# Adaptive-norm transformer pair on one core: TensorE's side stage ahead of the value products in each half step

## The reference

```python
# layer 0
score = (h @ Wq) @ (h @ Wk).T / sqrt(32);  causal, zero and masked -> float32 min
x = x + ga * softmax(score) @ (h @ Wvdown @ Wvup)
h = layernorm(x) * (1 + cb) + sb
x = x + gb * relu(h @ We[argmax expert] + be) * p       # one expert of 8 per token
# layer 1
q, k, v = h @ Wq.T, h @ Wk.T, h @ Wv.T                   # 16 heads of 8
x = x + ga * (softmax(q @ k.T * 8**-0.5) @ v @ Wout.T + bout)
x = x + gb * ((h @ W1.T + b1) @ W2.T + b2)
```

## Time and profile before

| | us |
|---|---|
| median of 3 runs | 1754.97 (1753.21 to 1757.65) |
| profiled execution, its own time | 1750.79 |
| span of its trace | 1749.5 |
| TensorE busy | 1605.5 |
| VectorE busy | 1491.2 |
| ScalarE busy | 1367.7 |
| GpSimd busy | 670.5 |

### The profile page before, as it was taken

How to read it: one execution, slowest core, us unless ns; L and a number is a source line. 1 busy time by engine, 2 the same in 40 slices (tenths; PEclk the granted TensorE clock), 3 DMA queues, 4 the chain that set the end, 5 groups by cost and what they waited for, 6 DMA issues and landing times.

```text
span 1749.5 us, 55041 instructions
## 1 busy us (share of the span) xinstructions
PE 1605.5 (92%) x23302; PEld 664.7 (38%) x23313; DVE 1491.2 (85%) x2256; ACT 1367.7 (78%) x1934; POOL 670.5 (38%) x1085
## 2 busy tenths in 40 slices
PE   5768999999999999999999999999999998998998
PEld 2543343334334343334334343334433343222224
DVE  4649988899889988899889988899888988998963
ACT  4443688887899778887898878897788878887884
POOL 2321345435534455335554264434554263002010
PEclk9899999999999999999999999999999999999999
DMA  2120211112210321112210321112111222101111
GB/s 72 51 65 25 63 39 41 35 54 61 67 50 17 96 65 42 30 44 75 66 48 19 82 65 52 34 40 83 45 40 35 60 59 66 35 25 50 36 29 32
DMA packets 83281, 87.10 MB, mean 50 GB/s; under 512 B 9452, under 2 KB 67484, under 8 KB 83036
## 3 DMA queue, kind: packets, MB, share of 16 engines
q1 hardware_dynamic: 82492, 83.07, 16.2%
q10 hardware_dynamic: 544, 0.52, 0.1%
HBM read 61.02 MB, written 21.99 MB: 47 GB/s over the span
## 4 chain that ended last, share of the span: by engine, by line
PE 59%; ACT 19%; DVE 13%; issue 5%; SPq 2%; DMA 1%; POOL 1%; ACTq 0%; POOLq 0%
PE pv_psum L836 20%; PE side_psum L564 14%; ACT p L1049 11%; PE buffer L821 11%; DVE row_max L1373 7%; PE buffer L811 7%; PE buffer L564 2%; PE side_psum L654 2%; PE side_psum L621 2%; SPq L539 2%; ACT s L965 1%; ACT o_sb L1058 1%; DVE st_f L1112 1%; DMA q_ops<-nm_rows 1%; ACT hT_b L1038 1%
## 5 line engine op out<-in xcount | busy, mean ns | idle before, releaser
L1373 DVE TENSOR_REDUCE row_max<-buffer 128x2 f32<-128x1024 f32 x1024 | 1234.0, 1219 | 142.8 <-PE buffer L811 132.0
L1049 ACT ACTIVATE p<-buffer 128x1024 f32<-128x1024 f32 x1024 | 1044.7, 1024 | 202.0 <-PE buffer L821 187.6
L836 PE MATMUL pv_psum<-p,v 128*9 128x256 f32 x8192 | 588.5, 384 | 10.6 <-ACT o_sb L1058 9.4
L811 PE MATMUL buffer<-k_ops,q_ops 24*128 24x512 f16 x2048 | 400.3, 388 | 34.0 <-ACT p L1049 25.0
L821 PE MATMUL buffer<-q_ops,k_ops 26*128 26x512 f16 x2048 | 400.7, 388 | 14.3 <-DVE row_max L1373 8.5
L836 PEld LDWEIGHTS pv_psum<-p,v 128*9 128x9 f32 x8192 | 150.4, 89 | 244.4 <-issue 161.4
L821 PEld LDWEIGHTS buffer<-q_ops,k_ops 26*128 26x128 f16 x2048 | 96.8, 91 | 382.2 <-issue 219.4
L1504 POOL TENSOR_TENSOR hm<-masks,hT_f 128x1024 f32<-128x1024 bf16 x56 | 120.3, 2148 | 102.3 <-PE side_psum L564 99.0
L811 PEld LDWEIGHTS buffer<-k_ops,q_ops 24*128 24x128 f16 x2048 | 96.8, 91 | 162.7 <-ACT p L1049 130.7
L1519 POOL TENSOR_SCALAR nm_parts<-nm 128x16 f16<-128x16 f32 x64 | 13.1, 205 | 293.9 <-DVE nm L1296 293.6
L564 PE MATMUL side_psum<-we,hm 128*32 128x128 f32 x3648 | 121.7, 275 | 2.7 <-issue 2.7
(11 more groups left out here) (309 smaller groups left out, 1621.1 us busy)
## 6 DMA issues: line engine op xcount, KB each, us to landing
masks<-masks_rows SPq DMA_DIRECT2D x16, 1024.0 KB, 6.4
q_ops<-products SPq DMA_DIRECT2D x256, 48.0 KB
k_ops<-products SPq DMA_DIRECT2D x256, 48.0 KB
attention<-o_sb SPq DMA_DIRECT2D x248, 18.0 KB
x<-in_L_attn_inputs SPq DMA_DIRECT2D x8, 512.0 KB, 4.4
products<-q_parts SPq DMA_DIRECT2D x16, 256.0 KB, 2.3
w_sb<-in_L_ffn_W SPq DMA_DIRECT2D x16, 256.0 KB, 3.0
out<-x SPq DMA_DIRECT2D x16, 256.0 KB, 2.5
```

Of the source, the lines that this page charges most:

```text
L811: m = e.matmul(buffer[:, hh, :], q_ops[rows, slot, of, i * P:(i + 1) * P], k_ops[rows, slot, of, halves(half)[1]], start=True, stop=True)
L836: m = e.matmul(pv_psum[q:q + VW, half * QUARTER:(half + 1) * QUARTER], v1[b % 2][:, kb, 2 * hp + hh, :], p_sb[n % KEPT][:, hh, part * QUAR ...
L1049: e.activation(p_sb[n % KEPT][:, :, :], unit("exp", n)[0][:, :, :], ACT.Exp, scale=over_scale[n // (2 * PERIOD)]).then_inc(S["exp_done"], 1)
L1373: e.tensor_reduce(mx[pair % 2][:, :, i, half], unit("max", n)[0][:, :, :], axis=AX.X, op=ALU.max).then_inc(S["max_done"], 1)
```

## The change

The loop over the half step's value products is moved from ahead of the side stage to behind it, on TensorE alone. No instruction is added or removed, and no wait changes.

```diff
             if h + 2 * LEAD < PAIRS * UNITS:
                 max_scores(h + 2 * LEAD)
-            for n in values_at.get(h, ()):
-                values(n)
             for name, *at in plan.get(h, ()):
                 if name in stages:
                     stages[name](*at)
+            for n in values_at.get(h, ()):
+                values(n)
             if h < 0:
                 keep_busy(1 if h < -LEAD else 3)
```

## The result

The changed kernel takes a median of 1778.95 us (1777.08 to 1779.76, 4 runs), the kernel before in the same session 1754.09 us (1748.60 to 1757.65, 4 runs). The ratio is 1.0143, with a 95% interval of 1.0115 to 1.0171: **slower by 1.4%, 25 us**. The profiled executions have spans of 1777.6 and 1749.5 us.

The account below looks back on a forecast made before the run. TensorE was taken to set the pace, with the chain scores, exponential, buffer release binding light half steps. Walked delays of 3.15 us a period, six periods, made 19 us: 1754.97 to 1774 us, range 1757 to 1802.

Parts of the forecast that it names:

- the one-hot term: One-hot transposes waiting 1.35 us for VectorE at 1173.28: values now come after them, +0.35 us a period.
- Part 1: TensorE's passes and mode switches in the new order: nothing added, zero; transposes-to-values taken at 0.58 us.
- Part 2: Side stages' waits that value products used to cover now delay values and scores: 65 us gross, partly absorbed.
- The first chain: Channel transposes at 1079.03, then `g0`: following scores walked at +0.43 us, then +0.32 behind `g0`.
- The gross account: Sum of all newly uncovered waits as if independent: 10.8 us a period, 65 us a run, an upper bound.
- The copy: ScalarE's copy of a pair's finished values, now late, holds up emptying and exponential: 0.3 us beyond the delay before it.
- The logits: Around 1161.41, transposes wait for VectorE, then a copy with an emptying behind it: +1.2 us a period.
- Layer-0 scores: Transposes and products from 1120 to 1152, alternating with waits of L811: +0.3 us a period, against 3.0 gross.
- The rest: Remaining places of the period (experts, output, first probabilities): +0.6 us a period.
- All waits exposed: Rival: nothing is absorbed, 65 us plus 24 copies at 0.4 us, 1830 us; above 1790 given 0.15.
- Absorbed: Rival: L811's 130.7 us of waiting for the exponential takes up all delay, time stays at 1755 us; chance 0.13.
- The earlier hand-over: Rival: ScalarE and VectorE get side products 0.43 to 0.85 us earlier, giving 1738 or 1748 us; faster given 0.10.

Follow-up runs that it names:

- e1: Kernel before, with the side stage ahead of the values only in the 118 half steps where it was ready when the values started; 1754.23 us, ratio 0.9993.
- e3: Kernel before, with the side stage first only in the 24 half steps in which a pair's values end; 1766.74 us, ratio 1.0063.
- e4: Kernel before, with the side stage first only in the 90 half steps with full-width transposes; 1760.11 us, ratio 1.0023.
- e6: Kernel before, with the side stage first in 295 of 319 half steps, all but the 24 where a pair's values end; 1770.43 us, ratio 1.0075.
- e7: Kernel before, side stage first in e1's set less its 6 half steps with a copy, plus 6 with layer 1 `channels`; 1748.50 us, ratio 0.9960.
- e2: Kernel before, with the side stage first only in the 201 half steps where it was not ready when the values started; 1781.98 us, ratio 1.0154.
- e5: Changed kernel, with ScalarE emptying the side bank before a pair's copy in 18 half steps; 1770.22 us, ratio 1.0082 to the kernel before.

## Why the prediction was right, point by point

**Predicted 1774 with 1757 to 1802, measured 1778.95.** The direction and the mechanism were right. The change itself was 25 us where I had 19. Part of that closeness is luck: the one-hot term, 0.35 for nothing, made up for more than a third of the 0.9 us a period by which the other terms were too small.

**Part 1, the passes: right.** The open pair, transposes-to-values, was taken at 0.58 from the earlier trace rows; it measured 1098.90 - 1098.32 = 0.58, so the bound below zero, a pair 0.32 us shorter (-29 us), is excluded. That agrees with the Trainium skill (TensorEngine Tiling (Array Packing), Key Properties), by which a change of tiling mode drains TensorE, but doesn't prove it: 0.42 of the 0.58 are the transposes' own weight loads, and no run here has transposes followed by a group of the same mode. For the other groups, e1 shows nothing for its 118 half steps, with an interval of -5 to +3 us.

**Part 2, waits no longer covered: right, and sized right where it was walked.** The first chain was walked at +0.43 and then +0.32. From the scores before the channels to those behind them the changed kernel takes 1099.45 - 1097.54 = 1.91 us; before, from 1078.15 to 1079.61, it was 1.46. That is +0.45. To the scores behind `g0` it is 3.80 against 3.43, +0.37. The gross account (65 us) would have had +0.81 there. Behind the next pair, walked at +0.53 and then +0.40, it was 0.61 and then 0.50. This step carries the prediction, and it is what kept the forecast from 1830.

**The copy: the mechanism right, the size too small.** I walked +0.3 beyond the delay before it and 0.45 at the second place. e3 measured 0.46 for each copy. In the walk the copy started at 1088.80, 0.04 us before the scores behind it (1088.44 + 0.40); in the trace it starts 0.14 after them (1108.47 against 1108.33), and everything behind ScalarE's copy moves by these 0.18 us. The step that was mis-sized is "about 1088.8" for the end of the pair's values; the delay that the scores brought along was 0.50 in place of 0.40. The place from channels to copy grew by 1.00, walked at 0.70. ScalarE's idle time before the copies grew by 8.7 us; I had put it at 10 to 20. I had also counted the costly places as two or three a period; there are four, and they hold 3.32 of the 3.75 us, with the stalls beside them.

**The logits, walked at +1.2: 1.27 measured.** Right. The wait itself, beside the earlier trace rows:

```profile
1182.33 0.68 DVE L1234 TENSOR_TENSOR xn_f<-side_psum,bg_rows 128x512 f32<-128x512 f32 x1
...
1183.06 0.42 PEld L654 LDWEIGHTS side_psum<-consts,s 128*128 128x128 f32 x4 [1.45 <-DVE xn_f L1234]
...
1183.65 0.12 PEld L836 LDWEIGHTS pv_psum<-p,v 128*9 128x9 f32 x8 [0.17 <-issue]
```

TensorE's wait for VectorE grew from 1.17 to 1.45 us, and the values stand behind it.

**The one-hot transposes, walked at +0.35: wrong, nothing measured.** The delay on TensorE is there: the scores start 0.32 us behind the transposes before and 0.76 after, 0.44 more, as walked. But it is not passed on. The same place of batch 5, in the kernel before:

```profile
972.86 0.21 PEld L685 LDWEIGHTS side_psum<-ident_bf,onehot 128*24 128x24 bf16 x4 [1.34 <-DVE x L1228]
...
973.18 0.09 PEld L821 LDWEIGHTS buffer<-q_ops,k_ops 26*128 26x128 f16 x2
...
973.85 0.48 DVE L1112 BATCH_NORM_STATS2 st_f<-x 128x6 f32<-128x128 f32 x2
```

and in the changed kernel:

```profile
991.84 0.21 PEld L685 LDWEIGHTS side_psum<-ident_bf,onehot 128*24 128x24 bf16 x4 [1.69 <-DVE x L1228]
...
992.60 0.09 PEld L821 LDWEIGHTS buffer<-q_ops,k_ops 26*128 26x128 f16 x2 [0.43 <-issue]
...
992.84 0.48 DVE L1112 BATCH_NORM_STATS2 st_f<-x 128x6 f32<-128x128 f32 x2
```

VectorE's next work starts 0.99 us behind the transposes before and 1.00 after. Through this place VectorE has no idle time and sets the pace; TensorE had slack: three half steps on, its scores are 0.28 later than before, and four on they are no longer late. I had walked TensorE and ScalarE there, not VectorE.

**Layer-0 scores, +0.3: undersized, 0.56. The rest, +0.6: undersized, about 0.9** (0.14 + 0.26 + 0.49). The 0.56 and the 0.49 are again places with a copy, which I had not walked as such; e3, with the copies alone, has 0.50 and 0.40 there. The sum of a period came to 3.75 where I had 3.15, all of it from the copies and from the terms that I had not walked in full, less the one-hot.

**The signs that I named.** Period +3 us: 3.75, inside the 1 to 6. L811's waits shrink: 130.7 to 116.2. The pair near 0.6: 0.58. "Idle ahead of side groups grows to 50 us or more": wrong in form. Summed over TensorE's side groups in the view of groups (all weight loads but the scores, the values and the filler of L846), it grew by 27.5 us, from 277.1 to 304.6. The idle time ahead of the scores grew by 42 (544.9 to 587.3), and that ahead of the values fell by 38 (244.4 to 206.5), since many values now follow a side stage directly. The idle time of a stall isn't all booked at the stage that stalls.

**The rivals.** All waits exposed (1830) is excluded by the time, and e4 beside e6 shows why at one place. Absorbed (1755) is excluded by the time; it holds at one place, the one-hot. The earlier hand-over, the other side, is excluded for the change as a whole, where the losses outweigh it and the new pair took 0.58. But its first half is real at one place, `channels_b`: e1 and e7 show 0.5 us a period there, some 3 us, under the 6.8 that I had set as its bound, and e7, which keeps it and avoids the losses, ends 7 us below before.

## What to carry to other kernels

An engine that works in order waits with everything that stands behind the waiting instruction. So put ready work ahead of work that may wait, and decide it place by place from the trace: the same swap cost 27 us where the side stage waited, nothing over all where it was ready, and gave 7 us once the half steps with a late copy were left out of those and six picked ones added. When an order changes on one engine, look at the orders of its consumers too; a copy whose input had become late held up a ready emptying, and turning the two round gave back 7 to 11 of 25 us. And walk a chain of stalls before summing it: here 10.8 us a period gross were 3.75 in the end.

## What the runs showed of the hardware

**A stretch of half clock, which I had not expected.** In the changed kernel the one-hot place of batch 6 is followed by a stretch in which the granted clock of TensorE is 1.2 GHz instead of 2.4. Windows of the trace (busy time of each engine, then the granted clock, DMA share and GB/s):

```profile
1190.00:1196.00 6.00, 4.50 (x85) 2.03 (x77) 5.42 (x13) 5.17 (x11) 0.00 (x0) 1.00 0.15 47
1196.00:1205.00 9.00, 9.00 (x84) 2.06 (x84) 8.28 (x15) 5.69 (x6) 3.17 (x7) 0.62 0.44 134
1205.00:1215.00 10.00, 9.48 (x131) 3.67 (x129) 9.01 (x14) 8.01 (x10) 2.93 (x6) 1.00 0.05 10
```

Ahead of it TensorE was busy for 4.50 of 6 us and waited 1.70 for VectorE; in the stretch it was busy throughout, and then the clock came back. This place of the period is 1.55 us longer than in the others. The same place has it in e1 (clock 0.76 over 1170 to 1184, 1.8 us longer), and in neither kernel in every period. From 200 us to the end of its trace, TensorE had 20.7 us at half clock in the profiled execution of before, 35.9 in that of the changed kernel, 24.2 in e1, 22.0 in e2 and 45.4 in e6, so the change isn't plainly its cause: e2 has the same long waits and little of it.

The stretches don't fall just anywhere. Between 200 and 1530 us the nine traces have 25 of them, and 24 begin at one of two points of the period: 11 one to three half steps behind that of the one-hot transposes, and 13 in the half step that is at 1120 us in batch 6, behind a `times_v`. At this second point no long wait stands ahead. In the kernel before, batch 4's:

```profile
704.00:716.60 12.60, 11.58 (x128) 4.40 (x124) 10.67 (x12) 12.05 (x22) 6.94 (x11) 1.00 0.20 60
716.60:720.00 3.40, 3.40 (x34) 1.06 (x36) 2.20 (x5) 1.26 (x3) 0.00 (x0) 0.50 0.18 59
```

TensorE was busy for 11.58 of the 12.6 us before, with no idle stretch above 0.4 us. So a long wait is not what it takes.

**It goes with the scatter of the runs.** Of the kernel before, measured beside e5 to e7, the runs with a mean clock of 0.983 or more took 1749 to 1752 us, those with 0.978 or less 1757 to 1763, and beside e1 to e4 1746 to 1753 and 1759 to 1764; of e7 the one at 0.985 took 1743.2 and the one at 0.978 1755.3. The run of e6 at 0.84 took 53 us more than the others; it has no trace. What sets a stretch off in one execution and not in the next stays open; no run here varied it by itself.
